# Strip sums and rank steps moved behind single units, the lightest strip first, source one-hots in pairs: a graph kernel on Trainium2

## The reference

```python
edge_index = stack([src, dst])
h = maximum(layernorm(x), 0)
x = x + gcn2(h, edge_index, W1, b1, W2, b2)        # two graph convolutions with self loops
h = maximum(layernorm(x), 0)
x = x + edge_layer(h, edge_index, edge_attr, W1, b1, W2, b2)

gcn_conv(x, W, b):  h = x @ W;  norm = dinv[src] * dinv[dst]
                    out = segment_sum(h[src] * norm, dst) + b
edge_layer:         msg = relu(concat(x[row], edge_attr) @ W1 + b1)
                    agg = segment_sum(msg, col) / max(count, 1)
                    relu(concat(x, agg) @ W2 + b2)
```

## Time and profile before

| | us |
|---|---|
| median of 3 runs | 2568.5 |
| lowest and highest run | 2562.87, 2580.36 |
| the profiled execution | 2580.26 |
| its span, first to last instruction | 2578.3 |
| count stage, first one-hot to last strip sum | 255.4 to 1041.6 |
| second convolution's sums end, message stage's first gather | about 1375, 1449 |

### The profile page before, as it was taken

How to read it: one execution, slowest core, us unless ns; L and a number is a source line. 1 busy time by engine, 2 the same in 40 slices (tenths; PEclk the granted TensorE clock), 3 DMA queues, 4 the chain that set the end, 5 groups by cost and what they waited for, 6 DMA issues and landing times.

```text
span 2578.3 us, 47552 instructions
## 1 busy us (share of the span) xinstructions
PE 2196.5 (85%) x15568; PEld 1825.4 (71%) x15569; DVE 1888.6 (73%) x3625; ACT 1217.9 (47%) x3289; POOL 1848.3 (72%) x1687
## 2 busy tenths in 40 slices
PE   0452689998999899599996699999999999999996
PEld 0131578997777788488885587778777877877875
DVE  6996998887887875644446577777777777777776
ACT  5841245665656676355553344334333433444440
POOL 1857777778888887777775477777767667777770
PEclk9766999999999999899998799999999999999998
DMA  9313033333333433278884244443434333434332
GB/s 367 145 46 122 21 121 130 122 122 120 120 125 120 170 121 130 77 273 326 311 310 160 85 121 121 116 123 98 124 111 138 97 120 113 124 112 122 116 90 60
DMA packets 127167, 357.85 MB, mean 139 GB/s; under 512 B 34082, under 2 KB 77831, under 8 KB 117687
## 3 DMA queue, kind: packets, MB, share of 16 engines
q10 hardware_dynamic: 24752, 186.56, 19.2%
q0 software_dynamic: 56880, 85.25, 12.8%
q1 hardware_dynamic: 45369, 84.00, 9.4%
HBM read 229.75 MB, written 125.93 MB: 138 GB/s over the span
## 4 chain that ended last, share of the span: by engine, by line
PE 66%; DVE 16%; DMA 5%; issue 5%; ACT 4%; POOL 3%; ACTq 0%; DVEq 0%; POOLq 0%; SPq 0%
PE ps_node L1056 6%; PE ps_feat L1056 6%; PE ps_sum L1161 6%; PE ps_node L1071 5%; PE ps_extra L1199 5%; PE ps_feat L1071 4%; DVE region_c L1988 4%; PE ps_node L1183 4%; PE ps_node L1187 3%; PE pre_banks L1044 3%; DMA rows_or_lows<-block_lows 3%; ACT rows L1275 3%; PE ps_feat L1183 3%; PE ps_sum L1187 3%; PE ps_sum L1183 3%
## 5 line engine op out<-in xcount | busy, mean ns | idle before, releaser
L790 POOL DMA_INDIRECT permuted<-rows_or_lows,slot_of_edge x768 | 929.1, 1210 | 234.0 <-issue 150.8
L772 POOL DMA_INDIRECT rows<-table,region_a x800 | 788.9, 986 | 330.4 <-issue 221.7
L1988 DVE TENSOR_TENSOR region_c<-iota_key,region_c 128x1568 bf16<-128x1568 f16 (+1 forms) x327 | 356.6, 1091 | 0.0
L1368 ACT ACTIVATE region_a<-pre_banks 128x392 bf16<-128x392 f32 x392 | 194.8, 497 | 245.6 <-PE pre_banks L1044 236.6
L1056 PE MATMUL ps_node<-region_a,region_b 128*128 128x256 bf16 (+1 forms) x1911 | 263.9, 269 | 0.0
L1056 PE MATMUL ps_feat<-region_a,region_b 128*128 128x256 bf16 x1764 | 251.9, 272 | 0.0
L556 DVE CAST wide_counts<-region_a 128x1024 fp32r<-128x1024 bf16 (+2 forms) x163 | 116.8, 722 | 156.1 <-PE ps_node L1071 65.4
L1199 PE MATMUL ps_extra<-msg_parts,target_hot 128*128 128x256 f32 x1176 | 222.8, 306 | 4.5 <-DVE msg_parts L2159 4.5
L554 ACT ACTIVATE wide_counts<-region_a 128x1024 fp32r<-128x1024 bf16 x150 | 158.4, 1060 | 120.3 <-PE ps_node L1071 55.4
L1161 PE MATMUL ps_sum<-onehot,rows 128*128 128x64 f32 x1600 | 210.6, 276 | 0.0
L1161 PEld LDWEIGHTS ps_sum<-onehot,rows 128*128 128x128 f32 x1600 | 205.8, 200 | 5.0 <-issue 3.8
(11 more groups left out here) (307 smaller groups left out, 4817.2 us busy)
## 6 DMA issues: line engine op xcount, KB each, us to landing
counts<-region_a ACTq DMA_DIRECT2D x23, 3136.0 KB
region_a<-counts ACTq DMA_DIRECT2D x11, 3200.0 KB
region_a<-counts ACTq DMA_DIRECT2D x11, 3072.0 KB, 11.8
rows_or_lows<-block_lows ACTq DMA_DIRECT2D x72, 448.0 KB
permuted<-region_b SPq DMA_DIRECT2D x25, 833.0 KB, 24.1
region_a<-permuted SPq DMA_DIRECT2D x24, 833.0 KB, 6.0
rows_or_lows<-edge_cols_in POOLq DMA_DIRECT2D x24, 544.0 KB, 4.3
region_a<-attr_t_in SPq DMA_DIRECT2D x50, 256.0 KB
```

Source lines behind the costliest of these rows:

```text
L772: nc.gpsimd.indirect_dma_start(rows[:, s, j * D:(j + 1) * D], None, tables[2], bass.IndirectOffsetOnAxis(ap=message_rows[:, c * TC + j:c * ...
L790: nc.gpsimd.indirect_dma_start(permuted, bass.IndirectOffsetOnAxis(ap=slot_of_edge[:, r * RT + k:r * RT + k + 1], axis=0), edge_rows_of[:, ...
L1368: nc.scalar.activation(counts[strip % 2][:, :, j * W:j * W + W], count_banks[w % BANKS][:, 0:KEYS].rearrange("p (d h) -> p h d", h=SB), AC ...
L1988: v.tensor_tensor(hot_key(u)[:, :, 0:n], iota_key[:, None, 0:n].to_broadcast([P, UNIT // SIDE, n, SIDE]), keys[:, :, None, :].to_broadcast ...
```

## The change

Four edits, all in the count stage. The order of the strips: `STRIP_AT` puts strip 22 first, then 0 to 21, then 23 and 24; sums and stores go to the true strip's place. Visits by position are then 64, 404, 201, 189, seven times 128 (positions 4 to 10), thirteen times 64 (whole in 11 to 16) and 28. The strip sum: in position s, `add_strip` of position s-2 stands behind the second unit, instead of that of s-1 behind the last. The late ranks: the steps stand behind single units (`LATE_STEPS`, in eighths of the strip's units), the scan is a step of its own with a semaphore `late_blocks` before it, and PE sums behind windows 12 and 22. They still run at positions 9 to 22. The source one-hots: a unit's buffer was laid out source by source with its eight visits side by side; it becomes four groups, each source by source with two visits side by side, as the keys already are. So PE's weights lie 4 bytes apart instead of 16.

```diff
--- before.py
+++ after.py
@@ -76,7 +76,9 @@
 LATE_READY_STRIP = 4
-LATE_SUMS_AT = (8, 16)
+ADD_BEHIND = 1
+LATE_SUMS_AT = (12, 22)
+LATE_STEPS = (1, 2, 6, 8)
 VISIT_ROWS_AT = 8
@@ -105,6 +107,9 @@
 SPLITS += (NW - len(SPLITS)) * [(1, 1)]
+STRIP_AT = [STRIPS - 3, *range(STRIPS - 3), STRIPS - 2, STRIPS - 1]
+WINDOW_AT = [w for strip in STRIP_AT for w in range(strip * SW, min(strip * SW + SW, NW))]
+SPLITS = [SPLITS[w] for w in WINDOW_AT]
 VISITS = [sum(k) for k in SPLITS]
@@ -262,7 +267,7 @@
         visit_lo = region_c[:, at_lo:at_src].bitcast(BF16)
-        hot_src = region_c[:, at_src:at_key].bitcast(BF16).rearrange("p (k s u) -> p k s u", k=2, u=UNIT)
+        hot_src = region_c[:, at_src:at_key].bitcast(BF16).rearrange("p (k g s i) -> p k g s i", k=2, g=UNIT // SIDE, i=SIDE)
         hot_keys = region_c[:, at_key:at_key + UNIT * KEYS].bitcast(BF16)
@@ -304,7 +309,7 @@
-        more_src = rows_or_lows[:, a:a + P * UNIT].bitcast(BF16).rearrange("p (k s u) -> p k s u", k=2, u=UNIT)
+        more_src = rows_or_lows[:, a:a + P * UNIT].bitcast(BF16).rearrange("p (k g s i) -> p k g s i", k=2, g=UNIT // SIDE, i=SIDE)
@@ -323,6 +328,7 @@
         zero_bf = sb("zero_bf", [P, P], BF16)
+        iota_side = iota_units[:].rearrange("p n u -> p (n u)")[:, 0:P * SIDE].rearrange("p (n i) -> p n i", i=SIDE)
         source_hot = [iota_units[:].rearrange("p n u -> p (n u)").bitcast(F32), slot_of_edge[:, 0:512].bitcast(F32)]
@@ -415,6 +421,7 @@
+        late_blocks = sem("late_blocks")
@@ -1041,7 +1048,7 @@
                         pe.wait_ge(C["hot"], u + 1)
-                    ins = mm(bank[:, part * n:part * n + n], hot_source(u)[:, :, j], hot_key(u)[:, j // SIDE, 0:n, j % SIDE], start=(k == 0),
+                    ins = mm(bank[:, part * n:part * n + n], hot_source(u)[:, j // SIDE, :, j % SIDE], hot_key(u)[:, j // SIDE, 0:n, j % SIDE], start=(k == 0),
                              stop=(k == SPLITS[w][part] - 1), skip_group_check=True)
@@ -1379,7 +1386,7 @@
                 act.wait_ge(C["evacuated"], strip * SW + (SW + BANKS))
-                act.dma_start(counts_dram[strip], counts[strip % 2].rearrange("p h d -> p (h d)")
+                act.dma_start(counts_dram[STRIP_AT[strip]], counts[strip % 2].rearrange("p h d -> p (h d)")
                               ).then_inc(C["stored_" + "ab"[strip % 2]], 16)
@@ -1555,7 +1562,7 @@
             v.tensor_copy(iota_key[:], key_iota.unsqueeze(2).to_broadcast([P, KEYS, SIDE]))
-            v.tensor_copy(iota_units[:], iota.unsqueeze(2).to_broadcast([P, P, UNIT]))
+            v.tensor_copy(iota_side, iota.unsqueeze(2).to_broadcast([P, P, SIDE]))
@@ -1641,13 +1648,15 @@
                 if step == 0:
-                    link(v.tensor_tensor(by_block(late_hot), by_block(late_iota), blocks[:, None, :].to_broadcast([P, SB, RT]), ALU.is_equal))
+                    v.tensor_tensor(by_block(late_hot), by_block(late_iota), blocks[:, None, :].to_broadcast([P, SB, RT]), ALU.is_equal).then_inc(late_blocks, 1)
+                if step == 1:
+                    dve.wait_ge(late_blocks, r - EARLY + 1)
                     v.tensor_tensor_scan(late_upto, late_follows, late_hot, 0.0, ALU.mult, ALU.add).then_inc(rank_hot, 1)
-                if step in (1, 2):
-                    for c in (2 * step - 2, 2 * step - 1):
+                if step in (2, 3):
+                    for c in (2 * step - 4, 2 * step - 3):
                         dve.wait_ge(rank_summed, r * n + c + 1)
                         v.tensor_reduce(late_most[:, :, c], most_of(ps_sum[c % 2], c), AX.X, ALU.max).then_inc(rank_taken, 1)
-                if step == 3:
+                if step == 4:
                     slots_of(r, r, late_most, late_slot, blocks)
@@ -1976,13 +1985,18 @@
-            def one_hots(windows):
-
-                for u in range(-(-visits_upto(windows[0]) // UNIT), -(-visits_upto(windows[-1] + 1) // UNIT)):
+            def units_of(windows):
+
+                return range(-(-visits_upto(windows[0]) // UNIT), -(-visits_upto(windows[-1] + 1) // UNIT))
+
+            def one_hots(units):
+
+                for u in units:
                     if BUILT_BEFORE[u]:
                         hold(C["built"], built_at(BUILT_BEFORE[u] * UNIT))
-                    v.tensor_tensor(hot_source(u), iota_units[:],
-                                    visit_lo[:, None, u * UNIT:(u + 1) * UNIT].to_broadcast([P, P, UNIT]), ALU.is_equal)
+                    lows = visit_lo[:, u * UNIT:(u + 1) * UNIT].rearrange("p (g i) -> p g i", i=SIDE)
+                    v.tensor_tensor(hot_source(u), iota_side[:, None, :, :].to_broadcast([P, UNIT // SIDE, P, SIDE]),
+                                    lows[:, :, None, :].to_broadcast([P, UNIT // SIDE, P, SIDE]), ALU.is_equal)
                     n = KEYS_OF_UNIT[u]
@@ -2004,7 +2018,7 @@
                 dve.wait_ge(applied[buf], strip // 2 + 1)
-                add_bank(strip, buf, width)
+                add_bank(STRIP_AT[strip], buf, width)
@@ -2018,18 +2032,22 @@
                     for strip in range(STRIPS):
-                        windows = windows_of(strip)
+                        units = units_of(windows_of(strip))
                         late = strip - LATE_STRIP + EARLY if LATE_STRIP <= strip < LATE_STRIP + RANGES - EARLY else None
-                        for j in range(0, len(windows), SEG):
-                            one_hots(windows[j:j + SEG])
-                            if late is not None:
-                                late_ranks(late, j // SEG)
+                        for j, u in enumerate(units):
+                            one_hots([u])
+                            if j == ADD_BEHIND and strip > 1:
+                                add_strip(strip - 2)
+                            for step, eighths in enumerate(LATE_STEPS):
+                                if late is not None and j + 1 == len(units) * eighths // 8:
+                                    late_ranks(late, step)
+                        if late is not None:
+                            late_ranks(late, 4)
                         if strip >= LATE_READY_STRIP:
...
                             dve.wait_ge(own_stored, 16)
-                        if strip:
-                            add_strip(strip - 1)
+                    add_strip(STRIPS - 2)
                     add_strip(STRIPS - 1, LAST_WIDTH)
@@ -2272,7 +2290,7 @@
     visit_of = np.zeros((3, VB * P), np.int32)
-    parts_of = [(w * W + j * (W // len(SPLITS[w])), k) for w in range(NW) for j, k in enumerate(SPLITS[w])]
+    parts_of = [(w * W + j * (W // len(splits)), k) for w, splits in zip(WINDOW_AT, SPLITS) for j, k in enumerate(splits)]
     target_of = np.concatenate([np.full(k, target) for target, k in parts_of])
```

## The result

| | before | after |
|---|---|---|
| median of the runs (4 each), us | 2574.43 | 2533.12 |
| lowest and highest | 2562.87, 2580.36 | 2532.41, 2535.55 |
| span of the profiled execution | 2578.3 | 2533.6 |
| count stage, first one-hot to last applied matmul | 785.9 | 750.5 |
| first to last gather of the message stage | 1070.6 | 1060.2 |

The ratio is 0.985, with a 95% interval of 0.981 to 0.989. The median is 2 us from the forecast of 2531, and the time lies within its range. The forecast started from the median of before that was known, 2568.5 of three runs; with a fourth it is 2574.43.

A forecast was written before the change was run, and what follows sets the result against it. Neither PE nor DVE is full, they take turns (DVE bounds strips 0 to 2 and 9). Gains of 15.4, 8.0, 2.3, -2, 13.8, 0.8, 2 and -1.5 make 38.8, rounded to 38: 2568.5 to 2531 us, range 2517 to 2552.

The forecast's parts named there:

- the strip after: Count stage, the strip following the six light ones, without ranks: 0.8 us gained.
- weights: PE's visits with the new one-hot layout: 2 us gained, between bounds of nothing and 12.
- Part 1: Strip sum moved behind the second unit: PE doesn't stall, so positions of 128 visits fall to 27.7 us.
- Part 2: Late rank steps: both stalls go in light positions, down to 23.2 us; whole windows lose 2 us for six.
- the chain: Whole windows: DVE's 17.2 us row from unit 7's wait through unit 2's signal, making unit 2 2.9 us late.
- Part 3: Strip order, strip 22 first: positions 0 to 3 take 164 us, gaining 15.4; positions 9 and 10 gain 2.3.
- Part 4: Source one-hot layout: no difference on DVE; load 146 to 97 ns, mostly hidden on PE, 2 us taken.
- rival D: Source one-hot on DVE loses its rate, 0.52 us more per unit, 118 us in all: 2649 us; chance 0.05.
- The clock: Granted clock, 0.92 in strip 9 before: a dip may come again, so 1.5 us set aside as loss.
- POOL: Scatters before the message stage: end at 1401 however short the stage is; gains up to about 48 us pass.
- Rival C: POOL shares its way with DVE, scatters end up to 15 us late, 5 us lost: 2536 us; chance 0.06.

The follow-up runs named there:

- the steps set apart: Changed kernel with late steps at eighths 1, 3, 5, 7 and PE's sums behind windows 14 and 22: count stage 729.3 us, whole program 2509.2 us.
- the split scan: Changed kernel with late scan in two halves, five steps, PE's sums behind windows 16 and 23, ranks from position 10: 2504.04 us, ratio 0.974 to the kernel before.
- four short one-hots: Changed kernel with each source one-hot made by four DVE instructions of 128x256 instead of one of 128x1024: count stage 794.5 us, 2858.2 us in all.
- two pieces: Changed kernel with each source one-hot made by two DVE instructions of 128x512 instead of one of 128x1024: count stage 763.0 us.

## Why the prediction was right, by its steps

**The sum by stretches held.** Against the earlier trace rows, in us gained:

| stretch | forecast | measured |
|---|---|---|
| positions 0 to 3 | 15.4 | 179.4 - 165.4 = 14.0 |
| positions 4 to 8 | 8.0 | 146.7 - 136.2 = 10.5 |
| positions 9 and 10 | 2.3 | 68.3 - 68.2 = 0.1 |
| whole windows | -2 | 188.2 - 191.8 = -3.6 |
| six light strips | 13.8 | 155.2 - 141.8 = 13.4 |
| the strip after | 0.8 | 22.5 - 21.6 = 0.9 |
| weights, clock | 2, -1.5 | in the rows above |
| together | 38.8 | 35.3, by the stage's length 35.4 |

**Part 1 was right, and was nearly all.** The two units ahead of the sum keep PE busy, and the strips fall to what PE's own work counts: 27.69 us against 27.7 and 23.12 against 23.2 with the sum moved alone; the weights make 27.24 and 22.95 of them. The sum's longest wait in the light positions of the changed kernel is 2.5 us, where up to 2 was forecast.

**Part 2 was half right.** That PE's wait for the scan goes, was right. That the new steps are what removes it, was right only for whole windows: with the sum moved alone, the wait was gone in the light strips too. In the whole ones the new steps were needed for it (with the rank steps of before put back, PE waits for the scan six times there, 14.6 us), but they put the stall at unit 2 in its place. With whole windows the chain was as written: unit 2 was due 9.8 us into the position and would be ready at 12.7, a stall of 2.9. The timeline of PE shows 2.6, from the end of three matmuls at 0.109 to the next visit, for whose unit DVE began the keys at 730.80:

```profile
729.77 0.49 PE L1063 MATMUL ps_feat<-region_a,region_b 128*128 128x256 bf16 x3
732.73 0.51 PE L1051 MATMUL ps_extra<-region_c,rows_or_lows 128*128 128x392 bf16 x2 [2.47 <-DVE region_c L2002]
```

The 31.6 counted for each is 31.5 in the positions at full clock. The forecast had the stall, and the steps set apart took it away. Its loss was put at 2 us for six positions; the two of 33.1 us, which read a clock of 0.95 where the others read 0.99 or 1.00, are the rest of the 3.6.

**Part 3 had the length of the stretch and not its worth.** The first position, to ACT's last evacuation at 272.7, took 17.3 us (forecast 17), and the next three to 420.8 took 148.1 (147). But the 15.4 was booked to the order against strip 22 at 25.9, and the moved sum alone takes that to 23.1 and strips 0 to 2 from 153.5 to 151.4. Its price was near what was counted: positions 9 and 10 give 0.1 us with a clock of 0.92 in the second of them, and 3.0 in the run without that dip, against 2.3 and 1.5 set aside for the clock. But the sum compared them with the old loops; in the new loops strips 3 to 9 would have been 6.3 us shorter in the old order, or 3.4 without the dip. Of this step the order itself kept 2.5 to 4.2 us, alone and on the kernel before 7.1. The parts don't add up: by themselves they give 34.5, -1.3, 7.1 and 6.1, together 46.4, and the change gives 35.4, so they overlap by 11. The old order in the changed kernel shows where 4.6 of that lie; in it the first strips have their lead from the sum's move already. Another 4.1 lie in the steps, which cost 1.3 alone and 5.4 in the changed kernel. Where the rest lies was not tried.

**Part 4.** The source one-hot keeps its rate: 0.682 us in the changed kernel, 0.685 before. Groups of the kernel after, by form:

```profile
L1063 PEld LDWEIGHTS ps_node<-region_a,region_b 128*128 128x128 bf16 x1911 | 176.2, 97 | 28.7 <-issue 1.5
L1998 DVE TENSOR_TENSOR region_c<-iota_units,region_c 128x1024 bf16<-128x1024 bf16 x164 | 111.8, 682 | 27.1 <-PE ps_turn L1051 24.2 <-PE pre_banks L1051 1.0 <-DVE consts L2118 0.3
...
L1051 PEld LDWEIGHTS pre_banks<-region_c,rows_or_lows 128*128 128x128 bf16 x686 | 63.5, 99 | 19.5 <-DVE region_c L2002 9.3 <-ACT region_a L1375 2.8 <-issue 1.3
```

The load falls from 146 to 99 ns, as forecast. Its worth was mis-sized: 2 us were taken, of a bound of 12, and the layout alone gave 6.1. In a strip of 128 visits it is 27.69 - 27.24 = 0.45 us, 3.5 ns a visit, of the 47 by which the load is shorter; the rest doesn't show in PE's time. Over positions 4 to 8 that makes 2.2 us, most of what they gave beyond the 8.0. By the rule of "Vector Engine (DVE) Microarchitecture Reference", section 5.2, in the Trainium skill, the new form would have cost an estimated 0.35 us a unit; this trace has none of it, so rival D stayed out. By "SBUF — State Buffer" of the Trainium skill, section "Door 1: The DMA port swizzle", with its 16-byte lines, the new load would be as short as the contiguous one; at 99 ns against 97 in this trace it is.

**The clock** was put at -1.5. The granted clock reads 0.92 in position 10, 0.98 and 0.94 in the stretches behind it, where the trace of before has strip 9 at 0.92 and 1.00 in those behind it. The repeat of the kernel shows that such a dip may be there or not at one place: position 10 was 2.9 us shorter without it. Whole positions of 33.1 us stand beside those of 31.5. Position 17 took 27.0 us at 0.94 in the changed kernel, in its repeat and in the old order, where the sum has 25.6; with the rank steps of before it took 24.5 at 1.00. So more was lost at a lower clock than the 1.5 set aside, and that is most of why 35.4 came and not 38.8.

**That the total is only 2 us off is in part luck.** The forecast took 38 from 2568.5. The measured medians, 2574.43 and 2533.12, differ by 41.3 us, and the stage gave 35.4 of them. From 2574.43 the same sum would have given 2536.4. That start and the stage's shortfall were made up by some 6 us gained outside the count stage, which nobody forecast; between the profiled executions it was the message stage that was shorter.

**POOL** ended at 1394.9, against "near 1400". It didn't hold up the message stage. That it ends at 1401 "however short the stage is" was wrong: with the split scan the last scatter began at 1384.5 and 1381.3. But the stage's length alone doesn't set it either. With the rank steps alone moved the stage was 787.2 us, longer than before, and yet the last scatter began 15 us sooner:

```profile
1385.05 0.95 POOL L796 DMA_INDIRECT permuted<-rows_or_lows,slot_of_edge  x1 [0.31 <-issue]
```

With the order alone (778.8 us) it began at 1408.5. In the changed kernel a scatter came every 1.51 us in positions 1 to 3, every 1.53 in 4 to 8, 1.84 with whole windows, 1.62 in 18 to 22, and every 1.29 to 1.39 behind the stage. So what DVE does beside it sets its pace as well as how long DVE does it; which of the two gave the 10 to 19 us in the kernels that ended early was not taken apart. Rival C's ground, that POOL shares its way with DVE, was right in a kernel that I hadn't thought of: with four short one-hots the wait for it is some 240 us.

## What to carry to other kernels

An operation that waits for another engine belongs behind as much ready work as the waiting engine's consumer can live on; here its place was worth 34.5 us of the 35.4, and no work was removed. When several edits work on the same turns between two engines, their worths alone don't add up, so book each against the kernel that has the others already. And where the buffers allow little lead, long operations of the other work are best set one by one between units: with them spread in that way the stage was 21 us shorter again, in one run.

## What the hardware showed that I hadn't expected

**POOL's indirect DMA takes its turn from DVE.** Where DVE runs source and key one-hots without a gap, POOL gets in one scatter per unit of DVE, whatever it could do by itself. Its pace was 1.49 us at a unit of 1.49, 1.56 at a unit of 1.56 (two pieces), and 1.26 with DVE quiet. With four pieces it didn't come in at all in 99.65 us, though DVE's longest operation there was the same 0.96 us. Thirteen scatters of that kernel stood for more than 5 us. While they stood, DVE ran nothing but one-hots, each reading both operands from SBUF, without a gap. Twelve of them ended at the first operation of another kind: a strip sum, which reads one operand from `agg` and one from the bank, a reduction of the bank, a conversion or a fill; the thirteenth ended while DVE waited. A gap on DVE isn't needed. The scatter here ended at 609.88, at a reduction that begins before the key one-hot has ended:

```profile
596.59 13.29 POOL L797 DMA_INDIRECT permuted<-rows_or_lows,slot_of_edge  x1 [0.30 <-issue]
...
608.08 0.97 DVE L2002 TENSOR_TENSOR region_c<-iota_key,region_c 128x1568 bf16<-128x1568 f16 x1
608.97 1.08 DVE L1658 TENSOR_REDUCE rows<-ps_sum 128x32 f32<-128x416 f32 x2
609.97 0.89 DVE L1999 TENSOR_TENSOR region_c<-iota_units,region_c 128x256 bf16<-128x256 bf16 x4
```

"SBUF — State Buffer" of the Trainium skill, section "Who interferes with whom", has a VectorE instruction with two SBUF inputs contend with a GpSimd instruction that reads SBUF, and one with at most one SBUF input not, outside VectorE's two-port modes. What ended the long scatters agrees; why two pieces let one scatter in per unit and four none, no run here shows.

**The message stage has its own variation**: 1070.6 us from first to last gather in the profiled run of before and 1055 to 1061 in eleven other traces, all but the two with source one-hots in pieces. The windows of the two stretches show the same DVE work, 780.1 and 779.0 us, and PE 7 us longer. Before and after:

```profile
1448.70:2519.30 1070.60, 1028.20 (x6932) 837.77 (x6933) 780.10 (x1714) 427.57 (x1227) 787.69 (x800) 0.97 0.39 114
```

```profile
1414.40:2474.60 1060.20, 1021.06 (x6922) 832.47 (x6923) 779.00 (x1712) 426.20 (x1225) 787.65 (x799) 0.97 0.39 114
```

What sets it was not tried.
